# A two-layer transformer kernel on one core: products behind the router's third source, factor and offset at the turned rows, new slots, and layer 1's head beside the tail

## What is computed

```python
x = x + attn0(cond0(x, cond_512, ...), ...)                  # 16 heads, causal, within-token head attention as "cond0" input
x = x + ffn0(cond2(x, itok, itok, mask, cond_512, ...), ...)  # router input: mlp_ln over six sources; 8 experts, top 2
x = x + attn1(cond1(x, cond_512, ...), ...)                  # down, relu, up, add; then attention with feature maps
x = x + ffn1(cond2b(x, cond_512, ...), ...)                  # generated weights; then an int8 product
def _mlp_ln(s, W1, b1, W2, b2, g, b):
    h = jax.nn.silu(s @ W1 + b1) @ W2 + b2
    return _ln(h, g, b)                                      # (h - mean) * rsqrt(var + eps) * g + b
```

## Time and profile before

| | us |
|---|---|
| median of 3 runs | 2657.68 (2648.51 to 2659.33) |
| the profiled execution, its own time | 2649.61 |
| its span | 2647.8 |
| TensorE / VectorE / ScalarE / GpSimd busy | 2096.1 / 1440.8 / 1025.5 / 852.6 |
| mean granted TensorE clock | 0.858 |

### The profile page before, as it was taken

The page is one execution under the profiler, slowest core; times in us unless marked ns, Lnnn a source line. Parts: engine busy times, 40 slices in busy tenths (PEclk is TensorE's granted clock), DMA queues, the critical chain, the costliest instruction groups (busy, mean ns, idle before and its releaser), DMA issues. The chain is left out here.

```text
span 2647.8 us, 33574 instructions
## 1 busy us (share of the span) xinstructions
PE 2096.1 (79%) x11774; PEld 1320.3 (50%) x11774; DVE 1440.8 (54%) x3634; ACT 1025.5 (39%) x2535; POOL 852.6 (32%) x586
## 2 busy tenths in 40 slices
PE   6427879878878868869869879699998596959697
PEld 5315545544445445545545545467787253535444
DVE  1357667767767767767767764422110255454635
ACT  2014535435535535535435435322222332515152
POOL 0253445245345345345345330221000241322321
PEclk9568889688878878879879879799999797979899
DMA  7100020030020020020020021224454211010200
GB/s 245 42 18 1 1 82 9 6 93 9 8 92 9 9 90 9 10 90 9 11 89 9 11 85 42 85 89 154 135 173 145 91 49 34 26 55 0 64 18 17
DMA packets 67456, 146.40 MB, mean 55 GB/s; under 512 B 16356, under 2 KB 42074, under 8 KB 62946
## 3 DMA queue, kind: packets, MB, share of 16 engines
q1 hardware_dynamic: 51434, 94.05, 10.4%
q0 software_dynamic: 15872, 50.35, 6.5%
HBM read 114.90 MB, written 29.46 MB: 55 GB/s over the span
## 5 line engine op out<-in xcount | busy, mean ns | idle before, releaser
L1195 ACT ACTIVATE att_buf<-att_buf,nmin 128x384 f32<-128x384 f32 (+3 forms) x512 | 287.3, 561 | 498.4 <-DVE nmin L1555 498.1
L1009 PE MATMUL bank<-kk,qT 32*128 32x512 f32 (+2 forms) x1024 | 324.4, 656 | 87.4 <-DVE nmin L1555 86.7
L771 POOL TENSOR_TENSOR big<-ex_at,kx 128x2048 f32<-128x2048 f32 x64 | 236.0, 3712 | 203.1 <-DVE xt_na L1307 132.0
L1036 PE MATMUL bank<-ident,att_buf 128*128 128x128 f32 x1280 | 233.6, 320 | 12.6 <-ACT att_buf L1203 11.8
L717 POOL TENSOR_TENSOR big<-kx 128x1280 f32<-128x1280 f32 x64 | 163.3, 2569 | 211.8 <-ACT kx L1110 149.0
L1050 PE MATMUL bank<-att_buf,vp 128*32 128x128 f32 x2560 | 221.0, 310 | 0.0
L1203 ACT COPY att_buf<-bank 128x384 f32<-128x384 f32 (+3 forms) x512 | 209.0, 408 | 25.0 <-PE bank L1050 20.5
L1544 DVE TENSOR_TENSOR att_buf<-bank,wdiag 128x128 f32<-128x128 f32 x384 | 93.0, 284 | 197.0 <-PE bank L1014 178.4
L1009 PEld LDWEIGHTS bank<-kk,qT 32*128 32x128 f32 x1024 | 110.3, 215 | 162.7 <-DVE nmin L1555 110.2
L1036 PEld LDWEIGHTS bank<-ident,att_buf 128*128 128x128 f32 x1280 | 172.4, 167 | 24.5 <-ACT att_buf L1195 18.0
L780 POOL DMA_INDIRECT buf_d<-nB,sidx x64 | 62.6, 978 | 334.5 <-DVE sidx L1429 317.4
(11 more groups left out here) (349 smaller groups left out, 4124.5 us busy)
## 6 DMA issues: line engine op xcount, KB each, us to landing
big<-in_eW SPq DMA_DIRECT2D x16, 1024.0 KB, 7.7
kk<-in_eW SPq DMA_DIRECT2D x16, 1024.0 KB, 8.0
buf_d<-zero SPq DMA_DIRECT2D x8, 640.0 KB, 7.9
xt_na<-in_xT SPq DMA_DIRECT2D x8, 512.0 KB, 3.4
nA<-in_xN SPq DMA_DIRECT2D x8, 512.0 KB, 7.9
x_d<-x SPq DMA_DIRECT2D x8, 512.0 KB, 3.8
...
```

The costliest lines, as they stand in the source:

```text
L771: pool.tensor_tensor(pv[:, c * P:(c + 1) * P, :].rearrange("p (h d) o -> p o h d", d=DH), spread(ex[:, t, :, 8 * c:8 * c + 8], 3, DH), spr ...
L1009: pe.matmul(bank[u % 2][:, 0:n], qT[r:r + 32, g, i * P:(i + 1) * P], kk[r:r + 32, g, T * i * P:T * i * P + n], start=True, stop=False)
L1036: mm = pe.transpose(bank[3 + u % 2][:, j * P:(j + 1) * P], pr[:, u % NPR, j * P:(j + 1) * P], ident[:])
L1195: act.activation(pr[:, u % NPR, 0:n], pr[:, u % NPR, 0:n], ACT.Exp, scale=-1.0, bias=nmin[:, u % 4:u % 4 + 1], accum_out=rsum[:, i, h:h + ...
```

## The change

1. GpSimd: `products(0)` and `products(1)` stand behind the work on source s, which in a trip now also waits for `h_ok` (VectorE's signal behind the second factor and offset). The addition of the offset to x moves behind the eight value products.
2. The router's last factor and offset, two VectorE operations on whole rows, are gone. They are applied as scale and bias per partition where turned rows are copied out of a bank: on ScalarE for the router's logits, in `rows_in` on VectorE for the experts (the rows that are scattered are without them).
3. New slots in `AT`.
4. In the iteration with the experts, steps due by slot `z` are taken before the first pair, which puts the first job's `rows_in` ahead of the router's first factor.
5. Layer 1: the head of the next pair runs in this pair's body, at stages OT, X3T and Y; the first pair's runs in the preparing block. x2 and yg have buffers of their own. Row numbers are made at QK, gathers issued at QK+1, combination and the weight products done at V; the SP queue fetches when GpSimd has read x2 for `xb`.
6. Layer 1: q and its squares in two ScalarE activations of 64 rows, not four of 32; weights are laid out anew for it.
7. Both loops are made with `hint_back_edge=True`, which puts a prefetch hint for the branch into each engine's program.

```diff
@@ -34,17 +34,18 @@
...
-      "kx": 0, "h1b": 1, "var2": 2, "sd2": 3, "t": 3, "t_out": 3, "h2": 4, "h2a": 6, "h2b": 8, "h": 10, "h_out": 11,
-      "s": 12, "s_out": 13, "u": 15, "silu": 28, "y": 30, "y_in": 34, "var3": 36, "sd3": 37, "f1": 38, "f2": 40, "f3": 42,
-      "f": 43, "f_out": 43, "r": 44, "r_in": 48, "r_exp": 49, "r_sum": 50, "pick": 51, "pos": 54, "place": 56, "rows": 60,
-      "sums": (6, 8, 11, 12, 14, 16, 18, 20), "full": 22, "sub": 24, "ex": 25, "den": 27, "pv": 28, "norm": 54,
+      "kx": 0, "h1b": 1, "var2": 2, "sd2": 3, "t": 3, "t_out": 3, "h2": 4, "h2a": 6, "h2b": 7, "h": 8, "h_out": 9,
+      "s": 11, "s_out": 12, "u": 14, "silu": 26, "y": 28, "y_in": 32, "var3": 36, "sd3": 37, "f1": 38,
+      "f": 40, "f_out": 41, "r": 42, "r_in": 46, "r_exp": 47, "r_sum": 48, "pick": 49, "pos": 52, "place": 54, "rows": 58,
+      "sums": (11, 12, 14, 15, 17, 18, 20, 21), "full": 23, "sub": 24, "ex": 25, "den": 27,
+      "pv": (30, 31, 34, 35, 37, 39, 40, 41, 43, 44, 46, 47, 49, 51, 53, 54), "norm": 55,
@@ -733,22 +735,21 @@
     gather(a["ms"], gac, 2)
+    for t in range(T):
+        pool.wait_ge(s(f"gath{t}"), 48)
     if b1 is not None:
-        pool.wait_ge(s("kx_dup"), 1)
-        products(0)
-    for t in range(T):
-        pool.wait_ge(s(f"gath{t}"), 48)
+        pool.wait_ge(s("h_ok"), 1)
     pool.tensor_tensor(ss, nA[:], ss, ALU.mult).then_inc(s("pool_own"), 1)
...
     if b1 is not None:
+        pool.wait_ge(s("kx_dup"), 1)
+        products(0)
         products(1)
...
         pool.dma_reset(range(s(f"gath{t}").num, s(f"gath{t}").num + 1))
-if b2 is not None:
-    pool.wait_ge(s("xn_in"), 16)
-    pool.tensor_tensor(xN[:], xN[:], spread(row("bout"), 1, T), ALU.add).then_inc(s("xb_ok"), 1)
 if b1 is not None:
@@ -772,6 +773,9 @@
+if b2 is not None:
+    pool.wait_ge(s("xn_in"), 16)
+    pool.tensor_tensor(xN[:], xN[:], spread(row("bout"), 1, T), ALU.add).then_inc(s("xb_ok"), 1)
 if b3 is not None:
@@ -856,7 +860,7 @@
-pe.wait_ge(s("f_ok"), 1)
+pe.wait_ge(s("f_ok"), T)
@@ -1159,7 +1163,8 @@
-act.copy(hT[:, m, :], bank[SIDE[m]][:]).then_inc(s("fT_ok"), 1)
+act.activation(hT[:, m, :], bank[SIDE[m]][:], ACT.Identity, bias=becol[:, m:m + 1],
+               scale=gcol[:, m:m + 1]).then_inc(s("fT_ok"), 1)
@@ -1371,9 +1376,7 @@
-normed(nB, nB, "sd3")
-yield AT["f2"]
-yield from affine(nB, nB[:], spread(row("g"), 1, T), spread(row("be"), 1, T), AT["f3"], "f_ok")
+normed(nB, nB, "sd3", "f_ok")
@@ -1434,7 +1437,8 @@
-dve.tensor_copy(eb[k % 2][:, m, 0:n], bank[m][:, 0:n]).then_inc(s("e_rT_ok"), 1)
+dve.tensor_scalar(eb[k % 2][:, m, 0:n], bank[m][:, 0:n], gcol[:, m:m + 1], becol[:, m:m + 1],
+                  ALU.mult, ALU.add).then_inc(s("e_rT_ok"), 1)
@@ -1567,6 +1571,7 @@
 advance(side, AT["var1"])
+advance(side, AT["z"]) if experts else None
 if b1 is not None:
@@ -1593,7 +1598,7 @@
-with nc.Fori(1, B - 1) as b:
+with nc.Fori(1, B - 1, hint_back_edge=True) as b:
@@ -1609,6 +1614,9 @@
+H_IN, H_DN, H_UP = ST_OT, ST_X3T, ST_Y
@@ -1708,6 +1717,65 @@
...
+def head_pe(pe, in_turn):
+    def lane(n, v, s):
+        bk = v["bank"]
+        yield H_IN
+        pe.wait_ge(s("x2_sum"), 2 * T)
+        if in_turn:
+            pe.wait_ge(s("o_ok"), K2)
+        for m in range(K2):
+            for t in range(T):
+                mm = pe.transpose(bk[m][:, t * P:(t + 1) * P], v["x2"][:, t, m * P:(m + 1) * P], ident[:])
+            mm.then_inc(s("xT_mm"), 1)
+        yield H_DN
+        pe.wait_ge(s("xT_ok"), 2)
+        pe.wait_ge(s("wud_ok"), 1)
+        for m in range(K2):
+            mm = pe.matmul(bk[0][0:M, :], v["wdn"][:, m, :], v["xT"][:, m, :], start=(m == 0), stop=(m == K2 - 1))
+        mm.then_inc(s("dn_mm"), 1)
+        yield H_UP
+        pe.wait_ge(s("dn_ok"), 1)
+        for m in range(K2):
+            pe.matmul(bk[m][:], v["wup"][:, m * P:(m + 1) * P], v["dT"][:], start=True, stop=True).then_inc(s("up_mm"), 1)
+    return lane
...
+def head_dve(dve):
+    def lane(n, v, s):
+        bk = v["bank"]
+        yield ST_V
+        dve.wait_ge(s("h_in"), 32)
+        dve.tensor_tensor(v["wdn"][:], dup[:], spread(v["dgb"][:, 0, :], 1, K2), ALU.mult).then_inc(s("wud_raw"), 1)
+        dve.tensor_tensor(v["wup"][:], upp[:], v["ugb"][:, 0, :], ALU.mult).then_inc(s("wud_raw"), 1)
+        dve.wait_ge(s("wud_raw"), 2)
+        dve.tensor_tensor(v["wdn"][:], v["wdn"][:], spread(v["dgb"][:, 1, :], 1, K2), ALU.add)
...
@@ -1758,16 +1836,15 @@
-    sp.wait_ge(s(f"kv_mm_{n}"), 1)
+    sp.wait_ge(s(f"xb_ok_{n}"), 1)
...
+    fetch_head(sp, v, lambda name, n=n: s(f"{name}_{n}"), LANES * b2 + LANES + n)
@@ -1777,19 +1854,19 @@
-yield ST_UP
+yield ST_QK
...
+yield ST_QK + 1
+if more:
+    gather_rows(pool, v, s)
...
-yield ST_O
-if more:
-    gather_rows(pool, v, s)
@@ -1924,19 +1988,12 @@
-in_stages(s, lane)
+in_stages(s, lane, *([head_pe(pe, True)] if more else []))
@@ -1944,8 +2001,8 @@
-for r, fn in ((0, ACT.Identity), (32, ACT.Square), (64, ACT.Identity), (96, ACT.Square)):
-    last = act.activation(v["qs"][r:r + 32, i - 2, :], src[r:r + 32, :], fn, bias=qscol[r:r + 32, i - 2:i - 1])
+for r, fn in ((0, ACT.Identity), (64, ACT.Square)):
+    last = act.activation(v["qs"][r:r + 64, i - 2, :], src[r:r + 64, :], fn, bias=qscol[r:r + 64, i - 2:i - 1])
@@ -1974,26 +2031,17 @@
 two = lambda bank: bank[:].rearrange("p (t f) -> p t f", t=2)
...
 yield ST_QK
+if more:
+    row_numbers(dve, v, s)
 for i in range(2):
...
 yield ST_V
+if more:
+    combine(dve, v, s)
 dve.wait_ge(s("v_mm"), 1)
@@ -2036,15 +2084,13 @@
-if more:
-    row_numbers(dve, v, s)
@@ -2077,10 +2122,10 @@
-with nc.Fori(0, B // LANES - 1) as b2:
+with nc.Fori(0, B // LANES - 1, hint_back_edge=True) as b2:
```

128 lines of the change are left out of this document (64 added, 64 removed).

## The result

The changed kernel takes 2525.85 us, the median of 4 runs (2514.43 to 2532.46); the kernel before, run beside it, 2653.1. The ratio is 0.9525, with a 95% interval of 0.9466 to 0.9584. A second set on another occasion gave 0.9523 (0.9457 to 0.9589). The forecast was 2440, with a range of 2385 to 2505: the direction held, but of the 210 us forecast only 127 came.

The account below looks back on a forecast made before the run. The prediction saw no engine full: a trip is a relay between TensorE, VectorE and ScalarE, so only TensorE's idle time was priced. Terms of -124.5, -12 and -73 took 2649.6 to 2440 us, range 2385 to 2505.

Parts of the forecast that it names:

- C: End of a layer 0 trip: picks, places and scatter two slots earlier save 2.6 us; seven ends, -18 us.
- Rival 2: The clock pays more: shorter waits lift a layer 0 trip's clock to 0.90; -64 us, 2376 us; chance 0.15.
- rival 3: The collision moves: VectorE's normalization and router picks meet denser value products, A and half of B lost; 2527 us; chance 0.06.
- A: Layer 0, GpSimd's products behind the third source: VectorE's second normalization no longer stretched; 6.5 us per trip, -39 us.
- B: Layer 0, router factor and offset: two VectorE operations go; 8 us per trip, -48 us.
- D: Layer 0 back-edge hint: TensorE's late start at later trips goes; 5.5 us at five back-edges, -27.5 us; layer 1 nothing.
- E: Layer 0, new neighbours: bias addition and last value product beside the router's picks cost 2 us per trip, +12 us.
- G: Layer 0's last iteration: copies ahead of the wait for gathered rows let the first expert's matmuls start earlier; -12 us.
- H to K: Layer 1: head off the front, tail with the head in it, fewer ScalarE query instructions, work in the middle; -73 us.
- K: Layer 1, middle of a body: gathers, combination and weight products there cost 4 us per body, +12 us.
- Rival 1: Layer 1 gives little: head steps land on the tail's chain, gathers hold key features; about -25 of 73, 2488 us; chance 0.15.

Follow-up runs that it names:

- control pair: Kernel with the router late from f on, plus eight float32 products ahead of the scores at units 38, 40 and 42: 8 columns 2587.91 us, 128 columns 2507.35 us.
- the pair with late slots: Changed kernel with the second half's slots as before: with the extra advance 2489.54 us (0.9376), without it 2493.12 us (0.9372).

## Why the prediction was wrong

*C and the slot table: the step that failed.* I priced the new slots at -2.6 us a trip, through the trip's end, and gave them no other cost. The first part failed: the scatter no longer ends last, but the stretch from the output projection to the next trip is 8.2 us as before, with the projection at half clock, so the gain was 0. The second failed by more: the router's steps from f on, two or three slots earlier, cost 8.1 us a trip: 190.3 against 182.2. That is 49 us for six trips, and 42 to 51 by the whole times. It is more than half of the 86 us that are missing.

*The clock.* My sum let the clock follow the idle time: idle less, and it gets better. Idle time fell by 14.8 us a trip, but over whole trips the time at 1.2 GHz stayed, 64 us before and 65 now; TensorE was idle in 17 us of it before and is in 3 now. Within the second half low time even went from 25 to 38 us. The gap behind which the clock falls was there before too (2.27 us at +134), and it fell there too; what changed is what TensorE does behind it. With the router's thin logits there the clock stays at 1.2 GHz for 31 to 34 us in four of six trips. The control pair shows that the width of the products matters. It is not the whole cause: in the first trip, and in four of six trips of layer 0's part alone, the same code shows no such stretch, and in the latter the trips still last 190 to 192, through waits. Why the early slots cost about as much in either form is open. Rival 2 (the clock pays more) and rival 3 (the collision moves) each had a part of this, with the wrong sign and with the wrong mechanism.

*A.* Right in kind. Undone, it costs 13.4 us a trip, not 6.5, but 6.7 of these lie at the trip's end, where six other programs have them too; the 6.7 that are left are what was forecast.

*B.* Right: 7.1 us a trip where I took 8, with the old slots around it.

*D.* Right in kind, for the late start of 3.3 us is gone, and right in giving layer 1 nothing. The price of 5.5 a back-edge is not shown: up to the first scatter a trip without the hint is only 0.6 us longer, with 3.9 more of idle time and 3.3 less of busy time.

*E.* The mechanism exists: two steps of 0.19 us take 3.4 us more a trip together. What that costs the trip stays open, and the 2 us that I took are neither shown nor refuted.

*G.* Too high: -12 forecast, -2.4 in the changed kernel's profile and -6 in the pair with late slots. I asked what the first copies waited for, and not what stood next in the same queue: the results' additions meet the same wait for gathered rows.

*H to K.* Right in sum: -70.5 against -73. A body lost 23.9 us (15.8 of head, 7.6 of tail by 51.87 - 44.23, the rest ScalarE's waits less K), the last body 16.3, and the preparing block grew by 17.4; the sum of the last two, +1.1, stood in my sum as -5 and ScalarE's share, -8 together, while the three bodies gave 71.7 and not 65: two errors that cancel, and so far luck. In six other programs a single body of the same code takes 127 to 131 us, which nothing here explains. Rival 1 is refuted.

*What is left.* With the late slots layer 0's trips still take 182.2 and not 177.5. Waits of 1.3 to 1.7 us on VectorE at +148 and +152 are part of it; I didn't take them apart further. Why the trip's end takes 23 to 25 us beside the scatter's transfers in seven programs with the new slots, and 17.7 in the changed kernel, also stays open. That the changed kernel is spared is luck: the prediction didn't ask for it.

The best version found is the change with the router's slots from f on left as they were: 2483.86 us, 0.9332 of before, and 2 percent below the changed kernel.
